# A list scheduler of three instruction streams gets new lengths for its items

## The reference

```
h = L0_tok(...)                      # state-space token mixer
h = layernorm(h + attn0(h))          # causal attention, 8 heads of 32, a rank-one bias on the scores
h = layernorm(h + ffn0(h))           # layernorm, full attention with 32 heads of 8, + x,
                                     # then 8 experts, each on a fixed part of the tokens: gelu(x w1 + b1) w2 + b2
h = layernorm(h + attn1(h))          # gated linear attention, 4 heads, silu gate, RMS norm
h = layernorm(h + ffn1(h))           # 8 experts, the top 2 of a softmax gate per token: relu(x W1 + b1) W2 + b2
```

## Time and profile before

| | |
|---|---|
| median of 3 runs | 1287.48 us (1284.52 to 1287.65) |
| the profiled execution's own time | 1279.39 us |
| its span, first to last instruction | 1277.7 us |
| TensorE busy in the span | 1074.6 us (84%), mean granted clock 0.906 |
| VectorE, ScalarE, GpSimd busy | 710.4, 472.6, 248.5 us |
| first attention slot's second score group | 119.7 us |
| last attention results, `p1_t` of pair 3 begins | 803.6 us |
| main loop's last real TensorE work (`gc` of pair 3) | 936.4 us |
| first matmul of `expert_mixture` | 955.2 us |

### The profile page before, as it was taken

One profiled execution on the slowest core, in us unless ns is written; L12 is line 12 of the kernel. 1 busy time (PEld: TensorE's weight loads), 2 busy tenths in 40 slices (PEclk: granted clock), 3 DMA queues, 4 the chain that ended last, 5 costly groups with the idle time before them and its releaser, 6 DMA issues. The chain is left out here.

```text
span 1277.7 us, 22878 instructions
## 1 busy us (share of the span) xinstructions
PE 1074.6 (84%) x8418; PEld 770.7 (60%) x8418; DVE 710.4 (56%) x1761; ACT 472.6 (37%) x938; POOL 248.5 (19%) x337
## 2 busy tenths in 40 slices
PE   1227997987899888989988988988989999999990
PEld 1124665544666456766455744773548999999980
DVE  7992444675555666747577655355443444444445
ACT  2111332444365443355533655433003333333332
POOL 3970000010000001201012100002132333333320
PEclk9857998988999899799987998888889999999995
DMA  5123241019521469022806220114921111111105
GB/s 172 18 52 110 84 168 49 18 33 166 68 75 66 195 215 107 31 79 67 165 1 88 88 67 1 33 34 161 375 91 34 43 35 38 39 34 43 35 30 201
DMA packets 73419, 108.88 MB, mean 85 GB/s; under 512 B 16592, under 2 KB 58336, under 8 KB 72864
## 3 DMA queue, kind: packets, MB, share of 16 engines
...
## 5 line engine op out<-in xcount | busy, mean ns | idle before, releaser
L1721 DVE TENSOR_REDUCE mx<-scores_ps 128x4 f32<-128x1024 f32 (+1 forms) x160 | 186.9, 1168 | 84.3 <-PE scores_ps L1193 44.0
L1549 ACT ACTIVATE pt<-turned_ps 128x1024 f32<-128x1024 f32 (+1 forms) x160 | 157.6, 985 | 146.8 <-PE turned_ps L1189 97.2
L2266 PEld LDWEIGHTS x_ps<-x_xtT,x_w1s 128*128 128x128 f32 x1248 | 145.3, 192 | 3.4 <-ACT x_xtT L2294 1.5
L2266 PE MATMUL x_ps<-x_xtT,x_w1s 128*128 128x128 f32 x1248 | 145.8, 275 | 1.0 <-ACT x_xtT L2294 1.0
L2280 PE MATMUL x_ps<-x_experts,x_hT 128*128 x624 | 141.0, 379 | 0.0
L2280 PEld LDWEIGHTS x_ps<-x_experts,x_hT 128*128 128x128 f32 x624 | 115.6, 190 | 14.2
L2309 ACT ACTIVATE x_hT<-x_ps,x_b1c 128x128 f32<-128x128 f32 x312 | 84.8, 382 | 16.6 <-issue 13.5
L1179 PE MATMUL turned_ps<-q,k 32*128 32x256 f32 x512 | 69.8, 348 | 22.4 <-DVE mx L1721 12.4
L1179 PEld LDWEIGHTS turned_ps<-q,k 32*128 32x128 f32 x512 | 42.3, 198 | 76.1 <-issue 40.6
L1064 POOL COPY vpad<-v 128x32 f32<-128x32 f32 x128 | 22.8, 223 | 311.2 <-PE ps L1230 296.4
L2329 DVE COPY x_w1s<-x_experts 128x2048 f32 x39 | 55.6, 1429 | 49.1 <-PE x_ps L2266 37.5
...
...
## 6 DMA issues: line engine op xcount, KB each, us to landing
...
```

The source lines that it names most:

```text
L1549: sc.activation(pt[v.index // 2 % (PT_RING // 2)][:, :, 0:wide], turned_ps[:, :, 0:wide], ACT.Exp)\
L1721: v.tensor_reduce(mx[:, u.group % 2, 0:blocks, u.n:u.n + 2].rearrange("p b n -> p n b"), scores_ps[:, :, 0:blocks * (P if u.causal else T) ...
L2266: last = mm(ps[2 * (i % 2) + f // KH][:, f % KH * P:(f % KH + 1) * P], w1s[:, i % 2, c, f * P:(f + 1) * P], xtT[:, i % 2, c, :], start=c = ...
```

## The change

Only the table of lengths changes. No item, no rule of `needs` and no instruction is added or removed. TensorE's length of nearly every item of streams a and b grows to about that of a matmul group in the trace, and so do those of an attention slot:

```diff
-        "Y3": [(.95, .7, .6, True, "h_t0 h_t1"), (1.75, 0, .6, True, "q0"), (1.75, .7, 0, False, "k0"),
+        "Y3": [(1.4, .7, .6, True, "h_t0 h_t1"), (1.9, 0, .6, True, "q0"), (1.9, .7, 0, False, "k0"),
...
-                 (1.75, .7, 3.2, False, f"up{e}3"), (.9, 0, 0, True, f"down{e}0+1"), (.9, 1, 0, False, ""),
+                 (1.9, .7, 3.2, False, f"up{e}3"), (1.9, 0, 0, True, f"down{e}0+1"), (1.9, 1, 0, False, ""),
...
-                (.9, 1.4, 0, True, "at0 at1"), (.9, 1.4, 0, False, "at2 at3"), (.9, 1.1, 0, False, "state"),
+                (1.7, 1.4, 0, True, "at0 at1"), (1.7, 1.4, 0, False, "at2 at3"), (1.6, 1.1, 0, False, "state"),
...
-                work["x"].append((2.4, 1.6, 1.6, True, "") if kind == "X0" else (1.65, 1.7, 1.6, True, ""))
+                work["x"].append((3.8, 1.6, 1.6, True, "") if kind == "X0" else (2.35, 1.7, 1.6, True, ""))
```

More of the change, by code:

```diff
@@ L593 @@
     STAGES = {
[L594 to L597 removed]
+        "Y3": [(1.4, .7, .6, True, "h_t0 h_t1"), (1.9, 0, .6, True, "q0"), (1.9, .7, 0, False, "k0"),
+               (1.9, 0, .6, False, "q1"), (1.9, .7, 0, False, "k1"), (1.9, 0, .6, False, "v0"),
+               (1.9, 0, .6, False, "v1")],
@@ L598 @@
+        "Y2": [(1.4, .7, .6, True, "p0_t0 p0_t1"), (1.9, 1.7, 0, True, "p0_0"), (1.9, 1.7, 0, False, "p0_1"),
                (0, 3, 0, True, ""), (0, 2.8, 0, True, ""), (0, 1.8, 0, True, ""),
-               (.95, .8, .8, True, "xn_t0 xn_t1")] +
-              [(1.75, .7, .6, n == 0, f"n{n}") for n in range(4)] +
-              [(1.75, 0, .6, False, "w0"), (1.75, 0, .6, False, "w1")] +
+               (1.4, .8, .8, True, "xn_t0 xn_t1")] +
+              [(1.9, .7, .6, n == 0, f"n{n}") for n in range(4)] +
+              [(1.9, 0, .6, False, "w0"), (1.9, 0, .6, False, "w1")] +
@@ L602 @@
               [(a, b, c, d, e.format(0)) for a, b, c, d, e in SPREAD],
-        "Y2d": [(.95, .7, .6, True, "p0_t0 p0_t1"), (1.75, 1.7, 0, True, "p0_0"), (1.75, 1.7, 0, False, "p0_1"),
+        "Y2d": [(1.4, .7, .6, True, "p0_t0 p0_t1"), (1.9, 1.7, 0, True, "p0_0"), (1.9, 1.7, 0, False, "p0_1"),
                 (0, 3, 0, True, ""), (0, 2.8, 0, True, ""), (0, 1.8, 0, True, ""),
-                (.95, .8, .8, True, "xn_t0 xn_t1")] +
-               [(1.75, .7, .6, n == 0, f"n{n}") for n in range(4)] +
-               [(1.75, 0, .6, False, "w0"), (1.75, 0, .6, False, "w1")],
+                (1.4, .8, .8, True, "xn_t0 xn_t1")] +
+               [(1.9, .7, .6, n == 0, f"n{n}") for n in range(4)] +
+               [(1.9, 0, .6, False, "w0"), (1.9, 0, .6, False, "w1")],
@@ L608 @@
         "Y2s": [(a, b, c, d, e.format(1)) for a, b, c, d, e in SPREAD],
-        "Y1a": [(.95, .7, .6, True, "p1_t0 p1_t1"), (1.75, .7, 0, True, "p1_0"), (1.75, .7, 0, False, "p1_1"),
-                (.95, .7, .6, True, "xf_t0 xf_t1")] +
+        "Y1a": [(1.4, .7, .6, True, "p1_t0 p1_t1"), (1.9, .7, 0, True, "p1_0"), (1.9, .7, 0, False, "p1_1"),
+                (1.4, .7, .6, True, "xf_t0 xf_t1")] +
                [slot for e in range(2) for slot in
-                [(1.75, .7, 0, True, f"up{e}0"), (1.75, .7, 3.2, False, f"up{e}1"), (1.75, .7, 0, False, f"up{e}2"),
-                 (1.75, .7, 3.2, False, f"up{e}3"), (.9, 0, 0, True, f"down{e}0+1"), (.9, 1, 0, False, ""),
-                 (.9, 0, 0, False, f"down{e}1+1"), (.9, 1, 0, False, "")]] +
+                [(1.9, .7, 0, True, f"up{e}0"), (1.9, .7, 3.2, False, f"up{e}1"), (1.9, .7, 0, False, f"up{e}2"),
+                 (1.9, .7, 3.2, False, f"up{e}3"), (1.9, 0, 0, True, f"down{e}0+1"), (1.9, 1, 0, False, ""),
+                 (1.9, 0, 0, False, f"down{e}1+1"), (1.9, 1, 0, False, "")]] +
@@ L615 @@
                [(0, 3, 0, True, ""), (0, 1.8, 0, True, "")],
[L616 to L619, removed]
-                (.9, 1.4, 0, True, "at0 at1"), (.9, 1.4, 0, False, "at2 at3"), (.9, 1.1, 0, False, "state"),
[L621 to L624, removed]
+        "Y1b": [(1.4, .7, .6, True, "h2_t0 h2_t1"),
+                (2.1, 0, .5, True, "u"), (1.05, 1.9, 0, True, "z"), (1.9, 0, 2.2, False, "vg0"),
+                (1.9, 2.5, .8, False, "vg1"), (1.9, 1.6, .8, False, "vg2"), (1.9, 0, 2.2, False, "vg3"),
+                (1.9, .8, 1.1, True, "gq"), (1.9, .8, 1.1, False, "gk"), (.3, 1.3, 1.5, True, "kt"),
+                (1.7, 1.4, 0, True, "at0 at1"), (1.7, 1.4, 0, False, "at2 at3"), (1.6, 1.1, 0, False, "state"),
+                (2.7, 1.3, 1.2, True, "o0"), (2.7, 0, 1.2, False, "o1"), (0, 1.5, 0, True, ""), (0, 2.2, 0, True, ""),
+                (0, 2.5, 0, True, ""), (1.4, .7, .6, True, "p2_t0 p2_t1"), (1.9, 1.7, 0, True, "p2_0"),
+                (1.9, 1.7, 0, False, "p2_1"), (0, 3, 0, True, ""), (0, 1.8, 0, True, ""),
+                (1.4, .7, .6, True, "gx_t0 gx_t1"), (2.5, 1.2, .6, True, "gs"), (0, 4.5, .5, True, ""),
```

## The result

The changed kernel is slower. Its four runs gave a median of 1312.46 us (1303.52 to 1317.27), four of the kernel before 1286.22 us (1284.52 to 1287.65): ratio 1.019, 95% interval 1.0163 to 1.0217. In a later comparison, with six and eleven runs, it was 1304.21 against 1286.87 us, ratio 1.0141, 1.0112 to 1.0171. So the change costs 18 to 24 us by these ratios; I had forecast 7.5 us and 1295 us. One execution among all runs, of `e2_middle`, took 2140 us, and it is left out of that kernel's ratio.

The account below looks back on a forecast made before the run. TensorE, 84% busy, bounds the kernel; from 803.64 us pair 3's chain, by VectorE and GpSimd. Terms sum to +7.5 us: 1279.39 becomes about 1287 profiled, 1295 us as median (8.1 above); range 1280 to 1306, own range 1291 to 1301.

Parts of the forecast that it names:

- slot 151 to `p1_t`: Slots 151 to 176: attention loses pair 2 work from a stretch where TensorE set the pace; -12.5 us, bounds -14 and -8.
- (1): From pair 3's `p1_t` to the `down` items' end: moved work and new bank waits; +7.3 us, bounds +3 and +9.
- (2): From the `down` items' end to `u`: gate items and their waits leave; -7 us, bounds -9 and -3.
- (3): From `u` to the end of pair 3's `o1`: takes in pair 2 items; +6 us, bounds +2 and +10.
- (4): From pair 3's `o1` to its `p2_t`: VectorE's queue delays the multiplications; +8.7 us, bounds +5 and +10.
- the signs that I had named: Profile after: last `p1_t` 9 to 10 us earlier, first expert matmul 5 to 10 us later, expert part unchanged.
- my own sign that the load was late: Expert part in the profile after: if it itself grows, the load of the experts was late.
- The DMA term: Main loop's end: later expert load runs beside pair 3's scatters and first gathers; +2 us, bounds 0 to 10.
- load in the way: Rival: pair 3's scatters land late beside the expert load; +15.5 us in all, 1303 us; chance 0.12.
- Slots 2 to 8: Early attention slots: two more bare slots, each waiting 1.05 us for VectorE's maxima; +2 us, bounds 0 and +4.
- Slots 9 to 144: Forecast as slots 71 to 151: even, except pair 1's adjacent `gs` and `gc`; +1 us, 3 either way.
- The rule on the clock: Tail: grouped work keeps TensorE's clock up, so it should gain, 8 us at most for half; counted little.

Follow-up runs that it names:

- e2_middle: Kernel before with the new order in slots 9 to 144 alone: 1284.16 us, ratio 0.9982 to the kernel before.
- e1_start: Kernel before with the new order in slots 2 to 8 alone: 1292.20 against 1288.98 us, ratio 1.0026.
- e13_load_late: Kernel before, old order, with one wait added on SP's queue so the expert load begins only after pair 3's `p2_t`: 1298.59 us, ratio 1.0072.
- e5_after_again: The changed kernel run once more without any edit: 1304.21 us, ratio 1.0141 to the kernel before.
- e3_tail: Kernel before up to slot 144, the new order from slot 145 on: 1303.95 us, ratio 1.0124 to the kernel before.
- e9_load_split: As e3_tail, but four experts' weights load in the main loop, the other four at the expert part's start: 1304.94 us, 1.0142 of the kernel before.
- e10_load_behind: As e9_load_split, but the last four experts' load waits until the first three tiles' rows are in place: 1298.21 us, 1.0069 of the kernel before.
- e12_at_late: As e8_work_late, but `vg2` to `kt` of pair 2 back in the slots; only `at0` to `at3`, `state`, `o0`, `o1` late: 1296.02 us, 1.0059 of before.
- e8_work_late: Old order to slot 144, then the changed kernel's, but pair 2's `gc` ahead of pair 3's `vg1`: 1296.29 us, 1.0083 of the kernel before.
- e7_gates_late: Kernel before, with only pair 2's `p2_t` to `gc` moved late, as in the changed kernel: 1295.60 us, ratio 1.0066 to the kernel before.

## Why the prediction was wrong

The direction was right and the size too small. The table has the lengths of each stretch in us, between the rows of the timelines that the prediction names. "Old" are the profiled executions of kernels with the old order there (before, `e1_start`, `e2_middle`, and `e13_load_late` up to `gc`), "new" those with the new tail (after, `e5_after_again`, `e3_tail`, and up to `gc` also `e9_load_split` and `e10_load_behind`); the difference is between the means.

| stretch | forecast | old | new | difference |
|---|---|---|---|---|
| slot 151 to `p1_t` | -12.5 | 87.9 to 90.0 | 76.6 to 80.0 | -10.5 |
| (1) to the end of the `down` items | +7.3 | 47.7 | 57.9 to 61.8 | +12.2 |
| (2) to `u` | -7 | 17.2 to 18.0 | 10.4 | -7.2 |
| (3) to the end of `o1` | +6 | 32.5 to 35.7 | 42.2 to 44.1 | +8.9 |
| (4) to `p2_t` | +8.7 | 8.3 | 16.4 to 17.8 | +8.9 |
| `p2_t` to `gc` | 0 | 19.8 to 23.8 | 19.5 to 20.1 | -1.9 |
| `gc` to the first expert matmul | +2 for the DMA | 18.6 to 18.8 | 22.0 to 22.5 | +3.5 |
| from there to the first tile | (in the same) | 5.2 to 6.6 | 8.5 to 8.6 | +2.8 |
| to the end | 0 | 317.0 to 318.6 | 318.3 to 318.6 | +0.9 |

Together, without the rounding, +17.7 us, where `e3_tail` measured 16 and I had 4.5.

Of the signs that I had named, `p1_t` came at 805.87 us, not 9 to 10 us ahead of 803.64, as slot 151 came 10 us later; the first expert matmul came 25 us later than 955.2, not 5 to 10; and from there to the end it took 326.9 us instead of 322.5, my own sign that the load was late.

**The DMA term** is the step that failed most. I took +2 from bounds of 0 and 10 "as two thirds of the load's shadow is over by then"; the old order with a late load costs 9.3 us. I had seen that the load would end at the loop's end and called it "just early enough" for the weights. The weights weren't late: in the expert part TensorE is nowhere seen to wait for them. Late were the small transfers on the path: pair 3's scatters, for which the loop's end waits (3.5 us), and the first gather (2.8 us). Both are gone in `e10_load_behind`. The Trainium skill says in "DMA: Bandwidth & Descriptors", section "Issuing engines are not separate DMA queues", that DMAs of scalar, sync and gpsimd interleave on the same 16 engines; the trace agrees, with a wait of 5.00 us for the gather where the load began again beside it, and none where it was held back. The rival "load in the way" was this mechanism, with a chance of 0.12, and its price of 10 us is nearer to the 9.3 measured, or to the 7.2 of the table's last three rows, than my 2.

**Stretch (1)** was mis-sized: +7.3 against +12.2, outside my bounds of +3 and +9. I had counted 4.4 us of new idle time; by the windows it is 6.1 (60.82 - 53.81 = 7.01, less 0.94), as I left out the waits ahead of `gq` (0.96) and behind `kt` (0.76), also places where items of a and b alternate. The rest is TensorE's busy time, 4 to 8 us more instead of 2.9, with the granted clock at 0.89 instead of 0.94. `e12_at_late` shows two sources of waits: the `at` groups, and the chain behind `p1_t` when `state` and `o0` no longer fill it. `e8_work_late` shows the step behind it: what the slots gave (11.4 us) came back whole in (1) (11.9).

**Stretch (4)** went nearly as predicted, (2) too: VectorE's queue, written out row by row, gave 8.7 and -7 for 8.9 and -7.2. In (4) there was some luck in the number. VectorE's multiplications ended 16.3 us behind `o1`, 8.1 later than before, in `after`, `e3_tail` and `e5_after_again` alike. What ended last was TensorE's own queue: the eight identity matmuls, which I had taken at 7.1 us, took 8.5 to 10.0 behind the wait of 5.4 us for `g_both`, and `p2_t` follows them without a gap. In `e3_tail`, first TensorE, then VectorE:

```profile
923.81 9.98 PE L1285 MATMUL scores_ps<-ident 128*128 128x512 f32 x16
933.62 1.04 PE L1295 MATMUL ps<-ident,ob 128*128 128x128 f32 x8
```

```profile
930.81 1.22 DVE L2000 TENSOR_TENSOR ob<-ob,yb_b 128x1024 f32<-128x1024 f32 x1
```

So 8.1 us are VectorE's order and 0 to 1.4 the identity matmuls at a lower clock. (3) took 3 us more than I had, within my bounds.

**Slots 2 to 8**: +2 forecast, 3.3 measured. The timelines show what I left out: from the third of the four waits on, TensorE's score matmuls take 1.65 us instead of 0.92, as at the low one of the clock's two levels. The granted clock over 115 to 150 us is 0.85 in all four kernels with the new order here. With the old order it was 1.00 only in the execution on which I predicted, and 0.90 to 0.95 in nine others, where two waits of 1.05 us stand in a row and a group of scores behind them took up to 1.65 us too (at 124.50 us in `e7_gates_late`). So the new order prolongs a fall of the clock that mostly comes anyway.

**Slots 9 to 144**: +1 with 3 either way; -2.3 measured, not told from none. The +1 for `gs` and `gc` of pair 1 came as forecast (4.41 - 2.97 = 1.4 us), and something else gave it back. The comparison of the two profiled executions suggested +4.5 here. Eight more executions with the old order took 215.0 to 215.7 us from slot 104 to slot 151; the one on which I predicted took 207.0. Most likely that is why it lay 8.1 us below the median. Five with the new order took 209.4 to 215.9, so that the spread belongs to neither order. Part of it can be seen: in `e13_load_late` TensorE waits 2.92 us for `tt_b` in two places (before 543.3 and 711.5 us), where the execution of before has no such wait. ScalarE and VectorE wait at the first of them too, until 542.2 us, for transposes that the trace shows ended at 539.2, and the trace names no releaser inside the kernel. What stops them is open.

**The rule on the clock.** Over the five windows what the clock fell short of full, length times one minus the clock, is 19.9 us before and 20.3 after. It shrank in (2) and behind `p2_t` and grew in (1), (3) and (4). TensorE's idle time in them rose from 13.9 to 24.5 us, so the gaps weren't filled, and the premise of the rule wasn't met. By the Trainium skill's "TensorE: Matmul & The Clock Gate", section "HAM oscillation — how this bites in real kernels", as I had read it in the prediction, the tail should have gained; these windows show no gain.
